# Mixing in natural image order with sorted writes, low-rank factors turned by TensorE, gating behind the mix, eight x tiles in flight, rare slots as a loop

## The reference, cut to what matters

```
y   = einsum('bct,bcd->bdt', x, cond_w[cond_id])          # the mix
h   = relu(layernorm(y @ gw1.T + gb1)); gates = h @ gw2.T + gb2
w   = softmax of the top 2 of 8 gates, zero where an expert is over capacity
out = y @ W0.T + ((y @ lora_A) * w) @ lora_B / 16         # main product and low-rank part
x1  = x + out
z   = x1 @ W1[adapter_id].T
s_g = mean(abs(w_gate)); s_u = mean(abs(w_up)); s_d = mean(abs(w_down))
out = x1 + bitlinear(bitlinear(z, w_gate) * bitlinear(z, w_up), w_down)
```

## Time and profile before

| | before |
|---|---|
| median of three runs | 1385.62 us |
| profiled execution, its own time | 1384.71 us |
| its span, first to last instruction | 1383.1 us |
| TensorE busy | 1331.9 us, 96% |
| first `main` product starts | 101.22 us |
| layer 1 starts (`linear`, slot 0) | 322.89 us |
| slot 16 done, first `gate_part` | 517.15 us, 523.07 us |

### The profile page before, as it was taken

The page is one execution under the profiler, slowest core; times in us unless marked ns, Lnnn a source line. Parts: engine busy times, 40 slices in busy tenths (PEclk is TensorE's granted clock), DMA queues, the critical chain, the costliest instruction groups (busy, mean ns, idle before and its releaser), DMA issues.

```text
span 1383.1 us, 24517 instructions
## 1 busy us (share of the span) xinstructions
PE 1331.9 (96%) x8864; PEld 853.0 (62%) x8865; DVE 744.2 (54%) x1154; ACT 372.8 (27%) x405; POOL 159.8 (12%) x118
## 2 busy tenths in 40 slices
PE   5889899979999998999999999999999999999998
PEld 5874444434444454555544788854888844888843
DVE  5467555434255555888855355573455582455521
ACT  3333344100111155888820011120111110111100
POOL 3200000000101000000000122220133310222210
PEclk9999999989999999999999999999999999999999
DMA  8644999979996937999874644354634455544354
GB/s 223 155 135 183 344 405 418 337 251 232 294 276 237 265 113 254 358 349 359 301 265 168 221 160 156 137 202 146 228 138 153 148 210 185 192 159 158 112 214 145
DMA packets 174337, 310.69 MB, mean 225 GB/s; under 512 B 99360, under 2 KB 131360, under 8 KB 166464
## 3 DMA queue, kind: packets, MB, share of 16 engines
q1 hardware_dynamic: 158352, 254.04, 56.1%
q10 hardware_dynamic: 11440, 32.69, 6.3%
q0 software_dynamic: 4480, 23.07, 4.8%
HBM read 220.78 MB, written 68.03 MB: 209 GB/s over the span
## 4 chain that ended last, share of the span: by engine, by line
PE 77%; DMA 8%; SPq 4%; issue 4%; DVE 4%; ACT 1%; POOL 1%; POOLq 0%; DVEq 0%; ACTq 0%
PE pair L1002 27%; PE pair L1039 17%; PE pair L862 13%; PE pair L918 10%; DMA region_q<-in_L_cond_weight 5%; PE pair L778 4%; PE pair L908 2%; DMA region_w<-in_L_ffn_w_gate 2%; SPq L475 2%; PE pair L745 2%; PE pair L675 1%; PE pair L733 1%; DMA region_q<-in_x 1%; SPq L360 1%; ACT region_q L1071 1%
## 5 line engine op out<-in xcount | busy, mean ns | idle before, releaser
L1002 PE MATMUL pair<-act_t,region_q 128*128 128x256 f16 x3696 | 404.1, 273 | 1.0 <-issue 1.0
L1002 PEld LDWEIGHTS pair<-act_t,region_q 128*128 128x128 f16 x3696 | 361.5, 98 | 43.7 <-issue 1.3
L1039 PE MATMUL pair<-region_q,region_w 128*128 128x512 f16 x1232 | 267.1, 379 | 1.3 <-DMA region_q<-wb_scratch 1.0
L1039 PEld LDWEIGHTS pair<-region_q,region_w 128*128 128x128 f16 x1232 | 120.2, 98 | 147.1 <-POOL region_w L660 1.8
L660 POOL TENSOR_TENSOR region_w<-region_q,region_w 128x1792 f32 (+1 forms) x33 | 118.4, 3587 | 524.2 <-ACT region_w L1258 524.2
L862 PE MATMUL pair<-region_w,act_t 128*128 x816 | 178.9, 379 | 0.0
L778 PE MATMUL pair<-region_w,act_t 128*128 128x512 f16 x768 | 173.9, 384 | 0.0
L918 PE MATMUL pair<-act_t,region_q 128*128 128x512 f16 x704 | 158.0, 383 | 5.9 <-issue 5.9
L862 PEld LDWEIGHTS pair<-region_w,act_t 128*128 x816 | 79.8, 98 | 92.7
L778 PEld LDWEIGHTS pair<-region_w,act_t 128*128 (+1 forms) x768 | 76.2, 99 | 89.2 <-issue 4.2
L1264 ACT ACTIVATE region_q<-pair 128x512 f32<-128x512 f32 x33 | 19.7, 597 | 400.4 <-PE pair L1002 400.4
(11 more groups left out here) (187 smaller groups left out, 1018.5 us busy)
## 6 DMA issues: line engine op xcount, KB each, us to landing
region_q<-wa_scratch SPq DMA_DIRECT2D x33, 1792.0 KB, 7.3
region_q<-wb_scratch SPq DMA_DIRECT2D x28, 1408.0 KB, 6.0
region_q<-in_L_cond_weight SPq DMA_DIRECT2D x40, 512.0 KB, 8.9
w1s_scratch<-region_q ACTq DMA_DIRECT2D x40, 512.0 KB, 8.1
wa_scratch<-region_q SPq DMA_DIRECT2D x22, 896.0 KB, 6.4
region_q<-in_x SPq DMA_DIRECT2D x64, 256.0 KB, 4.6
region_w<-in_L_ffn_w_gate SPq DMA_DIRECT2D x16, 688.0 KB, 5.6
wb_scratch<-region_q SPq DMA_DIRECT2D x11, 896.0 KB, 4.1
```

The lines of the kernel that those rows point to most:

```text
L1002: mm = pe.matmul(bank(s_bank, b)[:, (1 - h) * HALF:(2 - h) * HALF], ring_a[s][:, h, o_a, k], moving[a], start=(opens and h == 1 and k == 0 ...
L1039: mm = pe.matmul(bank(s_bank, b), iop[:, a, p, o_a, tp * P:(tp + 1) * P], ring_b[r][:, p], start=(opens and p == 0 and a == 0), stop=(not ...
```

## The change

Everything up to the first `main` is written anew, the sums of w_gate move, and the branch of the rare slots becomes a loop.

- x tiles are loaded in memory order, one transfer of 128 rows each, eight in flight (`load_mix`), with no need of the sorted places; the halves are written to the sorted places instead, as two instructions of 64 columns per chunk on each of ScalarE and VectorE (`y_part`, `low_y`, `halves_at`). W0 blocks come between them on the same queue.
- The first two tiles' small matrices are issued by ScalarE, the others by GpSimd, four register reads at a time (`fields`).
- lora_A is one transfer of 64 rows of 8 KB; 32 small matmuls put it in place (`turn_factors`, behind mix 6).
- All 16 mixes come first, over three PSUM pairs (`MIX_PAIR`), then all 16 gate products. Two of three rounds of the sort stand among the gates, and VectorE's gating behind the mix.
- w_gate is now 18 pieces of up to 1280 columns, loaded from ScalarE's queue and summed by ScalarE (`sum_gate`), from the gate products on.
- The rank 0 blocks 4 to 7 and their stores come later on ScalarE and VectorE; `residual(3)` comes ahead of `prep_low(1, 2)`, and x tiles 2 and 3 are loaded ahead of the eight blocks of rank 1.
- `optional` is gone; a `Fori` over slots 17 to 19 with an `If` inside stands between the two `gate_part`.

```diff
+NMIX = 8
+MIX_PAIR = (1, 0, 1, 0, 1, 0, 1, 0, 2, 1, 0, 2, 1, 0, 1, 2)
 # sync engine
+            def load_mix(t):
+                wait_if(sp, y_done, t - NMIX + 1)
+                sp.dma_start(mix_nat[t % NMIX], x_rows[t * P:(t + 1) * P, :]).then_inc(mix_loaded[t % NMIX], 16)
-            for k in range(KC):
-                sp.dma_start(lora_a_nat[:, k], lora_a[:, k * P:(k + 1) * P, :].rearrange("e i r -> i e r"))\
-                  .then_inc(lora_loaded, 16)
-                    for p in (GATE_LOADS[t] if isinstance(t, int) else ()):
-                        load_gate(p, p % 2, stat_gate)
+            for t in range(2, 4):
+                sp.wait_ge(acc_released, t - 1)
+                load_pair(x_nat[t - 2], x_loaded[t - 2], t)
 # TensorE
+                for h in range(2):
+                    picked = ident[0:E * KC, 0:E * KC].rearrange("p (e k) -> p k e", e=E)[:, 4 * h:4 * h + 4]
+                    for r in range(R):
+                        mm = pe.matmul(pair[3][:, h * H:(h + 1) * H].rearrange("p (n r) -> p r n", r=R)[:, r],
+                                       turned[:, r], picked, start=True, stop=True)
+            for t in range(NT):
+                mix(t)
+                if t < 4:
+                    prep_w0(t + 2)
+                if t == FACTORS_AT:
+                    turn_factors()
+            gate_part(0, 0, pair[0], 2)
+            linear_t(k - 1, 0)
             with pe.If(pairs > k):
-                linear(k, 1)
-                linear_t(k - 1, 0)
-                optional(k + 1, 0, pairs)
-                gate_up(0, 0)
+                with pe.Fori(k, NSLOT) as i:
+                    with pe.If(pairs > i):
+                        linear(i, 1)
+                        linear_t(i, 1)
+            gate_part(0, 0, pair[1], 0).then_inc(gu_done, 1)
 # ScalarE
+            def sum_gate(p):
+                cols = piece_cols(p)
+                tile = stat_gate[p % 2][:, 0:cols.stop - cols.start]
+                act.wait_ge(gate_loaded[p % 2], 16 * (p // 2) + 16)
+                act.activation(tile, tile, ACT.Abs, accum_out=stat_g[:, p:p + 1]).then_inc(gate_summed, 1)
+                if p + 2 < NPIECE_G:
+                    load_gate(p + 2)
+            for n in range(NT):
+                tmp_part(n)
+                if n in (6, 10, 14):
+                    gate_sqrt((n - 6) // 4)
+                if n % 2 == 1:
+                    sum_gate(n // 2)
+            for o in range(4):
+                store_w(o, o)
+            for p in range(13, NPIECE_G):
+                sum_gate(p)
+            rank0_part(4)
+            rank0_part(5)
 # VectorE
+            for quarter in range(3):
+                gate_moments(quarter)
+                gate_logits(quarter)
-            for t in range(10, NT):
-                residual(t, t % 2, pair[t % 2])
-                for p in GATE_PIECES[t]:
-                    v.wait_ge(gate_loaded[p % 2], 16 * (p // 2) + 16)
-                    v.tensor_reduce(stat_g[:, p:p + 1], stat_gate[p % 2], X, ALU.add,
-                                    apply_absolute_value=True).then_inc(gate_summed, 1)
-                prep_low(t // 2, t)
-                low_x1(t)
```

More of the change, by code:

```diff
@@ L728, in mix @@
-            def mix(t, slot, s, loads):
-                pe.wait_ge(mix_loaded[slot], loads)
-                pe.wait_ge(cond_loaded[slot], loads)
-                wait_if(pe, y_low, t - 1)
+            pe.wait_ge(index_sorted, 1)
+            ix_sum(pair[0][0:1, 0:NB], ix_part, ix_onehot)
+            ix_sum(pair[0][0:1, NB:2 * NB], ix_rank, ident[0:NB, 0:NB]).then_inc(index_sum, 1)
+            prep_w0(1)
+            def mix(t):
+                slot, s = t % NMIX, MIX_PAIR[t]
+                pe.wait_ge(mix_loaded[slot], 16 * (t // NMIX + 1))
+                pe.wait_ge(cond_first[t] if t < 2 else cond_loaded[t % 8], 32 * (t // 8 + 1 if t % 8 > 1 else 1))
+                if s in MIX_PAIR[:t]:
+                    pe.wait_ge(y_low, max(u for u in range(t) if MIX_PAIR[u] == s) + 1)
+                elif s == 0:
+                    pe.wait_ge(index_ready, 1)
+                elif s == 2:
+                    pe.wait_ge(ag_low, 1)
@@ L792, in turn_x1 @@
                 transpose8(pair[2], x1_nat[s], ident).then_inc(x1_transposed, 1)
-            pe.wait_ge(y_low, NT)
             pe.wait_ge(w_low, NPREP0)
-            for t in range(2):
-                for q in range(4):
-                    main(t, t, q)
+            for q in range(4):
+                main(0, 0, q)
+            pe.wait_ge(index_ready, INDEX_ALL)
+            pe.wait_ge(tmp_copied, NT)
+            for q in range(4):
+                main(1, 1, q)
             pe.wait_ge(count_ready, 1)
@@ L1174, in _ @@
             x1_part(0, 0)
+            store_w(4, 0)
+            store_w(5, 1)
+            rank0_part(6)
             x1_part(1, 1)
-            with act.Fori(1, NT // 2) as i:
+            rank0_part(7)
+            store_w(6, 2)
+            store_w(7, 3)
+            for s in range(2):
+                x1_part(2 + s, s)
+                prep_part(1, 2 + s)
+            with act.Fori(2, NT // 2) as i:
                 for s in range(2):
@@ new lines, in _ @@
+            low_w0(6)
+            low_w0(7)
+            v.wait_ge(index_sum, 2)
+            then(v.tensor_copy(ix_adps, ix_ps[0:NB, 96:97]))
+            then(v.tensor_scalar(ix_adps1, ix_adps, 1.0, None, ALU.add))
+            then(compare(ix_tmp, ix_ps[0:NB, 64:96], ix_adps, ALU.is_lt))
+            then(v.tensor_reduce(ix_first, ix_tmp, X, ALU.add))
+            then(v.tensor_tensor(ix_since, ix_part, ix_first, ALU.subtract))
+            then(v.tensor_copy(odd_i, ix_since))
+            then(v.tensor_scalar(odd_i, odd_i, 1, None, ALU.bitwise_and))
@@ L1864, in _ @@
             turn_a(1, 1)
-            optional(k, 1, pairs)
+            low_z(k - 1)
+            with v.If(pairs > k):
+                with v.Fori(k, NSLOT) as i:
+                    with v.If(pairs > i):
+                        copy_z(i, 1)
+                        low_z(i)
+            for j in range(k, NSLOT):
+                with v.If(pairs <= j):
+                    v.tensor_copy(cnt[0:1, 0, j - k:j - k + 1], out_c[0:1, :]).then_inc(z_low, 1)
             quantize(3, 1, 1)
```

481 lines of the change are left out of this document (214 added, 267 removed).

## The result

The changed kernel takes 1389.4 us in the median of 17 runs (1387.5 to 1390.9), the kernel before 1385.9 us beside it; the ratio is 1.0023 with a 95% interval of 1.0016 to 1.0031. The forecast was 1364 us, 21.6 us faster.

The account below looks back on a forecast made before the run. TensorE, busy 96% of the span, was taken as the bound, with transfers alongside it from 144 to 246 us (share 1.02). Weight stretch 3 + tail 11.1 + rare slots 7.5 = 21.6 us off 1385.6 gave 1364 us, range 1352 to 1375.

Parts of the forecast that it names:

- The start: Everything up to the first `main`: it starts at 85.5 us, 15.7 us ahead of 101.22.
- Index places and the first small matrices: Start: there at about 11 us; with 3 us excess and 10.8 us for four tiles, 24.8 us.
- Tiles 4 to 6: Start: they alternate two buffers at 2.2 us a tile, ending at 31.4 us.
- I take 0.2 us, 6.4 us in all, and 1 us for the eight gate transposes: Start, turning the factors: 32 small fp32 matmuls at 0.2 us each, plus the transposes, ending at 38.8 us.
- Nine tiles over three buffers: Start, remaining mixes: they go at TensorE's 1.83 us each, 16.5 us, ending at 55.3 us.
- The gating and the new wait: Behind the mix: low-rank turn at 114.3 us, VectorE's gating level at 116; `lora(0)` waits 10 us for ScalarE, until 128.5.
- The weight stretch: From x tile 2's load to rank 4's last low half: 2 us longer for moved stores, 3 us gained by tile 10.
- some 3 us: Weight stretch, a sign of being right: a TensorE wait of this size one tile after the old one at 161 us.
- Tail and slots: Layer 0's tail without VectorE's w_gate sums gains 11.1 us; the rare slots' shorter jump gains 7.5 us.
- x tile 13: Layer 0's tail: no wait seen; a rival kept the stall here, 8 of 11.1 us left standing, 1372 us, chance 0.08.
- "wrong" sign: Start: a first `main` beyond 95 us would mean mix tiles wait for x or for small matrices.
- the only slow one: Rival ahead of `lora(0)`: two w_gate pieces land in 20 and 17 us instead of 7 and 4, 1390 us; chance 0.06.

Follow-up runs that it names:

- the last run: Changed kernel with lora_A in eight transfers between x loads, w_gate sums spread, and places read two tiles at a time instead of four: 1363.7 us, ratio 0.9852.

## Why the prediction was wrong

**The start, which failed.** The first `main`, forecast at 85.5 us, came at 104.95. By its own steps:

- "Index places and the first small matrices should be there at about 11 us" and four tiles by 24.8: mix 4 started at 27.45. The first mix waited 4.15 us for a cond block and started at 14.60. **2.7 us.**
- Tiles 4 to 6, forecast 6.6 us, took 8.3: ScalarE and VectorE read the places of four tiles into registers at a time, and that held mix 6 for 2.20 us (0.85 in the last run). I had costed these reads at nothing. **1.7 us.**
- "I take 0.2 us, 6.4 us in all, and 1 us for the eight gate transposes": 14.7 us. A product took 0.44 us, outside both of my bounds, 0.11 and 0.23 us. The nearest rows had contiguous weights; at the full clock the stride of 64 bytes doubled the price. **7.3 us.** The stride is not all of it: contiguous weights would have taken back 2.9 us and no more, because the clock fell all the same, and the sum had no term for that.
- "Nine tiles over three buffers go at TensorE's 1.83 us": 21.9 us for 16.5. The half clock that the products left took 2.9 us of it (15.69 against 7 x 1.83), the register reads, with two issues of w_gate loads between ScalarE's halves, 2.44. **5.4 us.**
- The last halves 0.1, the gates 2.2. ScalarE waits for w_gate pieces between the copies of the gates' results, and TensorE's waits of 1.56 and 0.42 us are that. **2.3 us.**

Sum 19.4 of 19.5 us. The largest single cause is the turn of the factors, by the run without it 13.5 us at the first `main` where 6.4 had been counted.

**The gating and the new wait** were right in mechanism and size: 30.6 us from the first `main` to the low-rank turn (28.8 forecast), then a wait of 9.18 us (10), released as described; 43.4 us from the first `main` to `lora(0)` for 43.0. That this wait was avoidable, at 2.8 us in the stretch behind it, was not in the prediction.

**The weight stretch**: "I count 2 us" of the 5.2 us for the stores of blocks 4 to 7. It was 5.5: the bound, not my value. It began 1.9 us later behind `lora(0)` than forecast. The wait of "some 3 us" in it came as 5.16 us. That an earlier start is kept through it, which I had taken from its share of 1.02, holds for most of the gain: x tile 2 moved between 128 and 157 us, and the stretch stayed between 109.9 and 113.9 us. Some is lost: among the four rows with the sums in the changed kernel's place the stretch grew from 109.9 to 112.3 us while its start moved from 157.3 to 146.1. From its end to the first linear product it was 65.65 or 65.66 us in all nine rows of the table that keep the changed kernel's order there.

**Tail and slots** were right: 12.1 us for 11.1, 7.3 for 7.5. x tile 13 made no wait. The Trainium skill's rule on instruction fetch (page "Runtime: NRT & Kernel Launch", section Instruction fetch mechanics) fits as the prediction used it: the shortened jump shows no issue wait in the earlier trace rows's place, in the changed kernel and in the kernel before with the loop. That the distance is the cause is not shown, though. Both kernels also have 16 products and a transpose between the last slot and the branch, and no run has the one without the other.

The errors sum up: 19.5 + 0.4 + 1.9 + 3.5 - 1.0 + 0.2 = 24.5 us, against 24.3 us between the forecast span (1383.1 - 21.6) and the measured 1385.8. My "wrong" sign, a first `main` beyond 95 us, was the one that came. The reason I gave with it, mixes that wait for x or for small matrices, covers the first 2.7 us and not the rest. None of the rivals had the start late: the only slow one priced w_gate's two landings ahead of `lora(0)`, which took 7.9 and 2.0 us for 7 and 4.

## What to carry to other kernels

Before replacing a slow transfer by work on the busiest engine, find what the transfer costs there now: here some 1.6 us against 13.5. Price small matmuls by instructions and by how their weights lie, by the rows of loads with the same stride if there are any, and count register reads as work of the engine that makes them. Where one stretch is bound by transfers, its start time decides the end, so a wait just ahead of it is worth most of its length: 9.2 us of wait gave 8.8 us here. And before calling a milestone's shift the work of an edit, find how far two traces of the same program differ there.

## What was not expected of the hardware

- A strided fp32 weight load of 128 columns took 307 ns at granted clock 1.00 and at 0.50 alike; a contiguous one 183 and 330 ns.
- The granted clock fell to 0.50 while TensorE was busy without a gap on these small products, in all six traces that have them, and came back only 3 to 6 us into the mixes behind them. With full mixes in their place it stayed at 1.00 in four traces of five.
- A wait of 2.44 us was followed by half clock in six traces of ten (1.6 us lost over two mixes). The one wait of 1.09 us at the same place was not.
- Eight transfers of 64-byte rows issued in a row took 14.59 us to issue, 1.8 us each; with x loads between them the same transfers took 0.44 us each.
